# Causal-attention scores in row halves of the matmul array, with units taken in pairs over two PSUM banks

## The chip, the cores and the metric

The kernel runs on one core of a Trainium2 chip. The time is the device time of one execution in microseconds (us). Before the change three executions took 767.08, 772.93 and 774.23 us, median 772.93. Another execution was taken with the hardware profiler; it took 773.25 us, and the trace of it is what is read here.

## The reference

The input is `x`, 8 sequences of 512 tokens with 128 channels. Two layers follow each other, each of the form `x = x + s(xn) * silu(f(xn))` with `xn` the layernorm of `x`.

- First layer, `s`: causal attention with 16 heads of 8 channels. The latent forms of the weights fold, so that per head a score is `q . k / sqrt(8)` over 8 channels, a softmax over the keys up to the query follows, and the weighted sum of the values is the head's output. `f`: a mixture of 8 experts of 64 hidden channels (exact gelu), with the two best logits of each token as gates.
- Second layer, `s`: a recurrence over the tokens, `W = W - 0.01 (W k - v) k^T`, read with a query in each step, with its own layernorm, keys, values and queries. `f`: one matmul with the sign of the weight.

```python
attn = jnp.einsum('bhql,bkl->bhqk', q_lat, c_kv) / sqrt(hs)
attn = jnp.where(causal[None, None], attn, -jnp.inf)
attn = jax.nn.softmax(attn, axis=-1)
```

All is float32.

## The kernel before, in words

**Precision and the stacks.** The channels of q and k are split into three bf16 parts each. A score of a head is then one bf16 matmul whose contraction runs over 3 x 3 x 8 = 72 rows (each part of q against each part of k); these rows lie stacked in `qst` and `kst`, [128 rows, 16 heads, 512 tokens], two buffers each by the parity of the sequence. Rows 72 to 86 hold a coarse causal mask (of 32-token blocks) as products of two constant rows, and rows 96 to 98 hold ones in `kst` and, later, the negated row maximum in `qst`, again in three parts. The rows of a sequence get there over DRAM: q and k are written out from `parts` by SyncE (`write_parts`, pieces `q` and `k`), and read back by `load_stacks` in two halves of eight heads, 12 transfers each (issued at L445 for `qst` and L449 for `kst`). A half may be loaded once the exponential units that read the same buffer are far enough, and the wait for that stands on SyncE's queue.

**Two passes over the scores.** A pass computes the row maximum: `s_unit` (L804) takes rows 0 to 95 of the stacks, with 128 query tokens as weights and 128 or 256 keys as the moving side, and writes one 128x512 PSUM bank `ps_s`; `reduce` on VectorE (L1264) takes the maximum of it into `cand`. On the four units whose keys are the query block itself, four more matmuls (L808) add a triangular mask to the diagonal 32x32 blocks. `ps_s` has two banks, which units take by turns: the wait at the head of a unit is for the unit two before. When eight heads are through, `m_parts` and `m_rows` turn the maxima and bring them over DRAM into rows 96 to 98 of `qst`. The second pass, one sequence later, is `e_unit` (L786 writes the mask of the diagonal, L789 the score minus maximum over all 128 rows), transposed, so that keys lie on the partitions; ScalarE takes the exponential of a 128x512 bank of `ps_e` (L1069) into `prob`. `ps_e` also has two banks taken by turns.

**Values.** A group of four heads makes ten units of each pass, u = 0 to 9. Behind unit 3, 7 and 9 the values can be multiplied: `pv0`, `pv1` and `pv2` (L824) write 32 output rows for each of the four heads of `ps_v`, with a column of ones beside the values for the sum. Then `ps_v` is copied to `yT`, transposed back by `yt` (L831) into `ps_v`, and VectorE divides. There are four groups, called steps 0 to 3, so 40 units of each pass for a sequence.

**The order of the work.** Every engine runs its own instructions in the order that `run` and `iteration` (L336 to L361) give: for each step and each u, first `unit`, then the pieces that `PLAN` (L81) lists for it. In one iteration five sequences are in work: the projections and stack loads of the newest (`second`), the score pass and experts of the next (`nxt`), the exponentials, values and gating of the current (`cur`), and the second layer of the two before (`prev`, `older`). The last iteration has a plan of its own. The pieces of the second layer solve a triangular system by levels, `lev_a1`, `lev_d1` to `lev_d6` (L890 and L903; their results are copied by ScalarE at L1105, and multiplied by VectorE at L1319), go through the recurrence by blocks (`c_u`, `c_y`, `c_r`; L1338 is VectorE's step of `c_r`), and take their masks from GpSimd (L612, L614, L624; L1100 is the copy of the gram ahead of them). L1052 is the gelu of the experts. Between a piece on one engine and the piece on TensorE that waits for it lie whatever units the plan puts there. `prob` has ten buffers of 512 columns, one for each u.

```python
                for step in range(1 + max(at[0] for at in plan)):
                    for u in range(UNITS):
                        if step < GROUPS:
                            unit(cur, nxt, step, u)
                        for name in plan.get((step, u), []):
```

## Time and profile before

| | |
|---|---|
| median of three executions | 772.93 us |
| the profiled execution | 773.25 us, span 771.5 us |
| instructions | 14463 |
| TensorE, matmuls | 663.5 us busy, 86% |
| VectorE | 448.1 us, 58% |
| ScalarE | 369.3 us, 48% |
| GpSimd | 234.9 us, 30% |
| chain that ended last | TensorE 64%, VectorE 17%, DMA 6%, no wait that the profile shows 4%, ScalarE 4%, GpSimd 3% |
| read from and written to memory | 24.44 and 9.96 MB |

The profile is a page of totals over the whole span, and the trace behind it can be asked for windows, timelines and groups. Engines are called PE (TensorE matmul), PEld (its weight loads, which run beside it), DVE (VectorE), ACT (ScalarE), POOL (GpSimd) and SP (SyncE). A row of the costliest groups has the line of the program, the engine, the operation, out<-in, the number, then busy us, mean ns of one, and the idle time of the engine just before with what ended it. Matmuls are pipelined and their ends are modelled, so that what one holds the engine for is read from the start of the one behind it. The row of twelve or more instructions that a timeline gives as one spans from the start of the first to the end of the last.

### The profile page before, as it was taken

To read this page: it belongs to the slowest core of one execution; us is meant where nothing else is said; L and a number is where in the kernel's file an instruction comes from. 1 tells how busy PE (TensorE), PEld (TensorE's weight loads), DVE (VectorE), ACT (ScalarE), POOL (GpSimd) and SP (SyncE) were. 2 spreads that over 40 slices of the span, in tenths; PEclk is the share of its full clock that TensorE was granted. 3 is DMA by queue.
4 is the path that set the end of the run, shared out by engine and by line. 5 is a ranking of instruction groups with operands and counts; after the bars stand their busy time and mean duration, and the time that the engine had idled before them with its cause. 6 is when DMAs were issued, how large, how long until landed. Compare 5 with 4: busy or idle time off the path is not lost.

```text
span 771.5 us, 14463 instructions
## 1 busy us (share of the span) xinstructions
PE 663.5 (86%) x5682; PEld 458.5 (59%) x5734; DVE 448.1 (58%) x1044; ACT 369.3 (48%) x688; POOL 234.9 (30%) x356
## 2 busy tenths in 40 slices
PE   4177698979999899989998999899998998896875
PEld 2034365537666676657665876576666775555663
DVE  5466357555857576576758575758575654425331
ACT  3502346744556455644556455645564556571210
POOL 5703001222333153124404331423331502224431
PEclk9999889979999999999999999999999999999995
DMA  2732730450035102530044004400341000000000
GB/s 71 135 62 53 120 58 8 98 95 7 8 82 97 36 1 66 88 68 1 28 100 85 8 7 103 105 7 7 87 87 27 2 7 15 21 2 0 1 14 14
DMA packets 31283, 36.31 MB, mean 47 GB/s; under 512 B 4385, under 2 KB 26512, under 8 KB 31216
## 3 DMA queue, kind: packets, MB, share of 16 engines
q1 hardware_dynamic: 31216, 35.39, 22.1%
q8 instruction: 45, 0.74, 0.4%
q14 instruction: 22, 0.18, 0.1%
HBM read 24.44 MB, written 9.96 MB: 45 GB/s over the span
## 4 chain that ended last, share of the span: by engine, by line
PE 64%; DVE 17%; DMA 6%; issue 4%; ACT 4%; POOL 3%; SPq 2%; another core or an unknown queue 0%; POOLq 0%; DVEq 0%; ACTq 0%
PE ps_s L804 8%; PE ps_v L824 8%; PE ps_e L789 5%; DVE cand L1264 5%; DMA kst<-split_scratch 4%; PE ps_a L749 4%; PE ps_e L786 4%; PE ps_c L890 3%; PE ps_c L903 3%; PE ps_a L738 3%; PE ps_a L713 3%; PE ps_s L808 2%; DVE stats L1195 2%; PE ps_c L907 2%; DVE second L1209 2%
## 5 line engine op out<-in xcount | busy, mean ns | idle before, releaser
L1264 DVE TENSOR_REDUCE cand<-ps_s 128x4 f32<-128x512 f32 (+1 forms) x320 | 212.9, 683 | 94.0 <-PE ps_s L808 73.8
L1069 ACT ACTIVATE prob<-ps_e 128x512 f32<-128x512 f32 x320 | 188.2, 597 | 136.8 <-PE ps_e L789 97.2
L804 PE MATMUL ps_s<-kst,qst 96*128 96x128 bf16 (+1 forms) x1024 | 134.2, 249 | 41.8 <-DMA kst<-split_scratch 23.6
L804 PEld LDWEIGHTS ps_s<-kst,qst 96*128 96x128 bf16 x1024 | 81.0, 105 | 100.7 <-issue 52.4
L789 PE MATMUL ps_e<-qst,kst 128*128 128x128 bf16 (+3 forms) x460 | 104.5, 296 | 0.0
L824 PE MATMUL ps_v<-prob,vaug 128*32 128x512 f32 (+3 forms) x1024 | 89.0, 443 | 0.3
L786 PE MATMUL ps_e<-identb,negmask 128*128 128x256 bf16 (+1 forms) x320 | 83.3, 260 | 6.0 <-ACT prob L1069 5.8
L624 POOL TENSOR_TENSOR second<-second,upmask 128x512 f32<-128x512 f32 x42 | 53.1, 1274 | 34.6 <-PE ps_c L890 34.6
L789 PEld LDWEIGHTS ps_e<-qst,kst 128*128 128x128 bf16 x512 | 50.6, 99 | 5.6 <-issue 0.3
L587 POOL CAST mparts<-nm 128x32 bf16<-128x32 f32 x16 | 3.4, 212 | 157.9 <-DVE nm L1271 157.9
L890 PE MATMUL ps_c<-second 128*128 128x128 f32 x336 | 46.0, 280 | 1.0 <-DVE second L1319 1.0
L786 PEld LDWEIGHTS ps_e<-identb,negmask 128*128 128x128 bf16 x320 | 31.2, 97 | 23.0 <-ACT prob L1069 11.9
L890 PEld LDWEIGHTS ps_c<-second 128*128 128x128 f32 x336 | 41.7, 191 | 4.4 <-DVE second L1319 1.8
L824 PEld LDWEIGHTS ps_v<-prob,vaug 128*32 128x32 f32 x1024 | 23.5, 108 | 31.1 <-issue 23.5
L903 PE MATMUL ps_c<-second 128*128 128x128 f32 x280 | 38.5, 281 | 2.9 <-ACT second L1105 2.2
L903 PEld LDWEIGHTS ps_c<-second 128*128 128x128 f32 x280 | 34.8, 191 | 9.1 <-issue 6.3
L612 POOL TENSOR_TENSOR second<-second,lowmask 128x512 f32<-128x512 f32 x7 | 8.9, 1273 | 101.0 <-ACT second L1100 101.0
L738 PE MATMUL ps_a<-xnT,w1s 128*128 128x512 f32 x64 | 36.9, 659 | 0.7 <-DVE krest L1215 0.3
L749 PE MATMUL ps_a<-w2s,hid 128*128 128x128 f32 x256 | 35.3, 281 | 1.0 <-ACT mrow L1061 1.0
L1048 ACT ACTIVATE hid<-ps_a,vecT 128x512 f32<-128x512 f32 x32 | 22.0, 688 | 24.0 <-PE ps_a L738 24.0
L749 PEld LDWEIGHTS ps_a<-w2s,hid 128*128 128x128 f32 x256 | 31.4, 191 | 1.7 <-ACT mrow L1061 1.7
L808 PE MATMUL ps_s<-negmask,identb 32*32 32x128 bf16 x512 | 31.4, 236 | 0.0
(301 smaller groups left out, 1076.6 us busy)
## 6 DMA issues: line engine op xcount, KB each, us to landing
qst<-split_scratch SPq DMA_DIRECT2D x48, 192.0 KB
kst<-split_scratch SPq DMA_DIRECT2D x144, 64.0 KB
split_scratch<-qparts SPq DMA_DIRECT2D x8, 384.0 KB, 2.5
split_scratch<-kparts SPq DMA_DIRECT2D x8, 384.0 KB, 2.5
xn<-in_L_attn_x_dram SPq DMA_DIRECT2D x8, 256.0 KB, 3.1
x_res<-in_L_attn_x_dram SPq DMA_DIRECT2D x8, 256.0 KB, 6.8
out_dram<-second SPq DMA_DIRECT2D x7, 256.0 KB, 2.4
max_scratch<-mrow SPq DMA_DIRECT2D x16, 96.0 KB, 1.7
```

The lines of the kernel that those rows point to most:

```text
L624: g.tensor_tensor(r.pair_up[lv % 2][:, :, :], r.gram[:, :, :], bcast(upmask[:, lv, :], 1, NT), ALU.mult)\
L738: mm(ps_a[:, :], w1s[:, 2 * c:2 * c + 2, :].rearrange("p e f -> p (e f)"), xnT[b.parity][:, :], start=True, stop=True)\
L749: mm(ps_a[:, tok(i)], hid[:, c, tok(i)], w2s[:, c, :], start=(i == 0 and c == 0), stop=False, skip_group_check=True)
L786: mm(diag, negmask[:, :], bcast(identb[:, :], 1, len(todo)), start=True, stop=False, skip_group_check=True)
L789: last = mm(ps_e[:, bank, at:at + TOK - P * j], k[:, hd, tok(j)], q[:, hd, P * j:TOK], start=False, stop=True, skip_group_check=True)
L804: last = mm(ps_s[:, bank, w * n:w * (n + 1)], q[0:MAXROW, hd, tok(i)], k[0:MAXROW, hd, keys[0]:keys[1]], start=(n == 0), stop=True, skip_g ...
L808: last = mm(ps_s[lo:lo + FINE, bank, :].rearrange("p (a c) -> p a c", a=GH)[:, :, lo:lo + FINE], identb[0:FINE, 0:FINE], bcast(negmask[0:F ...
L824: last = mm(ps_v[32 * hh:32 * hh + 32, P * j:TOK], vaug[:, j, GH * grp + hh, :], prob[:, u, o:o + TOK - P * j], start=(j == 0), stop=(j == ...
L890: last = mm(r.ps_c0[:, tok(i)], r.pair_up[lv % 2][:, i, :], r.inv[:, i, :], start=True, stop=True)
L903: last = mm(r.ps_c0[:, tok(i)], r.invT[:, i, :], r.ablk[:, i, :], start=True, stop=True)
L1069: af(prob[:, u, :], ps_e[:, u % 2, :], ACT.Exp).then_inc(S["e_emptied"], 1)
L1264: vec.tensor_reduce(cand[:, i, h0:h0 + len(hds), S_SLOT[u]], ps_s[:, u % 2, :].rearrange("p (a c) -> p a c", a=len(hds)), AX_X, ALU.max)\
```

## The change

Scores of the row-maximum pass no longer take the coarse mask rows, so 72 rows of contraction remain; 64 of them are given to one half of the array's rows and the other 8 dropped from the pass (they stay in the stacks for the second pass). The 16 heads are split into two sides. A head of side 0 has its rows from row 0 up, a head of side 1 from row 64 up and around (`(64 + 8 * pair) % 128`), and the matmul of the pass contracts rows 0 to 63 for side 0 and 64 to 127 for side 1. A pair of units, one for four heads of side 0 and one for four heads of side 1, fills the two banks of `ps_s` with matmuls that alternate between the sides, and one reduction reads both banks. The pass has 20 pairs for a sequence instead of 40 units. The diagonal mask is added as two matmuls of 64 rows for each side and bank (`half_of`), over 64 or 128 columns of four heads, with constants that are also stored with their halves swapped (`ident_swap`, `neg_swap`, four transfers at the start).

The second pass goes in pairs too: `e_pair` fills both banks of `ps_e`, over all 128 rows, and one exponential reads both. For both passes the wait at the head of a pair is for the pair before. A fill of `ps_v` holds eight heads: each group of 32 output rows takes a head of side 0 and then one of side 1 of the same rows, whose weights have their values in other columns (0 to 8 and 16 to 24 of the 32). So there are two fills, six pieces and two `yt` for a sequence. Pairs run at even u only, and the plan puts the pieces anew. `load_stacks` has 25 transfers for a half instead of 12, of half the bytes or less; the loads of the row maxima are two for a half instead of one. The value copy on ScalarE is two copies, and `prob` has 6 buffers of 1024 columns.

In the diff the lines that are taken out of `load_stacks`, `e_unit`, `s_unit`, `pv` and `yt` are left out, since the kernel before is printed above.

```diff
-PAIRS = PARTS * PARTS * HD
-FINE = 32
 MAXROW = 96
+HALF = P // 2
 HALF_HEADS = 8
-GROUPS, GH = 4, 4
-UNITS = 10
+FILLS, SIDES, GH = 2, 2, 4
+FH, FW = 8, 16
+STEPS, UNITS = 4, 10
+UNIT_PAIRS = FILLS * UNITS
+PROB_RING = 6
+ONES_AT = (96, 32)
 ONES = 1 + 0x3F80 / 2 ** 23
...
 PLAN = {
     (0, 0): ["c_y2"], (0, 1): ["c_r3", "gb0"], (0, 2): ["ln2_stats", "c_u3"], (0, 3): ["c_y3"], (0, 4): ["gb1", "ln2_norm"],
-    (0, 6): ["pv0", "c_xn2t", "ln3_stats", "c_out", "gb2"], (0, 7): ["ln3_norm"], (0, 8): ["gb3"], (0, 9): ["pv1", "c_ht"],
-    (1, 0): ["load_x", "c_kt", "c_qt", "m_rows1"], (1, 1): ["c_vk", "out"], (1, 2): ["c_gram", "pv2"], (1, 3): ["logits"],
-    (1, 4): ["yt", "c_ffn", "gates"], (1, 5): ["lev_a1"], (1, 6): ["pv0"], (1, 7): ["lev_d1"], (1, 8): ["gt"],
-    (1, 9): ["pv1", "lev_a2"], (2, 0): ["ln1_stats", "lev_d2", "m_parts0"], (2, 2): ["ln1_norm", "lev_a3", "pv2"], (2, 3): ["lev_d3"],
-    (2, 4): ["yt", "m_rows0", "zero"], (2, 5): ["lev_a4", "xnt"], (2, 6): ["pv0", "q", "lev_d4"], (2, 8): ["lev_a5", "k"],
-    (2, 9): ["pv1", "lev_d5"], (3, 0): ["stacks0", "h0"], (3, 1): ["lev_a6"], (3, 2): ["h1", "lev_d6", "pv2"], (3, 3): ["c_u0"],
-    (3, 4): ["h2", "yt", "c_y0"], (3, 5): ["c_r1"], (3, 6): ["pv0", "c_u1"], (3, 7): ["c_y1", "h3"], (3, 8): ["c_r2"],
-    (3, 9): ["pv1", "c_u2"], (4, 0): ["m_parts1", "gelu", "stacks1"], (4, 1): ["pv2"], (4, 2): ["v"], (4, 3): ["yt", "x1"],
+    (0, 6): ["c_xn2t", "ln3_stats", "c_out", "gb2"], (0, 7): ["ln3_norm"], (0, 8): ["pv0", "gb3"], (0, 9): ["c_ht"],
+    (1, 0): ["load_x", "c_kt", "c_qt", "m_rows1"], (1, 1): ["c_vk", "out"], (1, 2): ["c_gram"], (1, 3): ["logits"],
+    (1, 4): ["c_ffn", "gates"], (1, 5): ["lev_a1"], (1, 6): ["pv1"], (1, 7): ["lev_d1"], (1, 8): ["gt"],
+    (1, 9): ["lev_a2"], (2, 0): ["pv2", "ln1_stats", "lev_d2", "m_parts0"], (2, 2): ["yt", "ln1_norm", "lev_a3"], (2, 3): ["lev_d3"],
+    (2, 4): ["m_rows0", "zero"], (2, 5): ["lev_a4", "xnt"], (2, 6): ["q", "lev_d4"], (2, 8): ["pv0", "lev_a5", "k"],
+    (2, 9): ["lev_d5"], (3, 0): ["stacks0", "h0"], (3, 1): ["lev_a6"], (3, 2): ["h1", "lev_d6"], (3, 3): ["c_u0"],
+    (3, 4): ["h2", "c_y0"], (3, 5): ["c_r1"], (3, 6): ["pv1", "c_u1"], (3, 7): ["c_y1", "h3"], (3, 8): ["c_r2"],
+    (3, 9): ["c_u2"], (4, 0): ["pv2", "m_parts1", "gelu", "stacks1"], (4, 2): ["v"], (4, 3): ["yt", "x1"],
 }
 LAST_PLAN = {
     (0, 0): ["last:zero_state", "c_y2"], (0, 1): ["c_r3"], (0, 2): ["gb0", "ln2_stats", "c_u3"], (0, 3): ["c_y3"], (0, 4): ["gb1"],
...
+def head_of(fill, side, hh):
+    return FH * fill + SIDES * hh + side
+def slot_of(fill, side, hh):
+    return HALF_HEADS * side + GH * fill + hh
+def low_rows(side):
+    return slice(HALF * side, HALF * side + HALF)
...
             def iteration(second, nxt, cur, prev, older, plan=PLAN):
                 for step in range(1 + max(at[0] for at in plan)):
                     for u in range(UNITS):
-                        if step < GROUPS:
-                            unit(cur, nxt, step, u)
+                        if step < STEPS and u % 2 == 0:
+                            unit(cur, nxt, step // 2, UNITS // 2 * (step % 2) + u // 2)
...
                                 if name in ("pv0", "pv1"):
-                                    pieces[name](of, step)
+                                    pieces[name](of, step // 2)
                                 elif name in ("pv2", "yt"):
-                                    pieces[name](of, step - 1)
+                                    pieces[name](of, (step - 1) // 2)
...
+            for dst, src in ((ident_swap, identb), (neg_swap, negmask)):
+                for side in range(SIDES):
+                    sp.dma_start(dst[low_rows(side), :], src[low_rows(1 - side), :]).then_inc(S["swap_loaded"], 16)
...
             def load_stacks(b, half):
...
                 loaded = S[f"stack_loaded{half}"]
...
+                sp.wait_ge(S[f"stack_zeroed{b.parity}"], 6)
+                after(sp, S["e_filled"], b.count(UNIT_PAIRS, UNIT_PAIRS * (half - 3) // 2))
                 sp.wait_ge(S["scratch_written"], b.count(32, 32))
...
+                q_rows = scratch[0].rearrange("r (d h) q -> (r d) (h q)", d=HD)
+                k_rows = scratch[1].rearrange("r (d h) q -> (r d) (h q)", d=HD)
                 n3 = PARTS * HD
...
+                for side in range(SIDES):
+                    s0 = slot_of(half, side, 0)
+                    heads, span = slice(s0, s0 + GH), slice(TOK * s0, TOK * (s0 + GH))
+                    for lo, n, first in STACK_ROWS[side]:
+                        sp.dma_start(qst[b.parity][lo:lo + n, heads, :].rearrange("p h q -> p (h q)"), q_rows[first:first + n, span],
                                      max_dma_last_dim=4096).then_inc(loaded, 16)
+                    for pair in range(PARTS * PARTS):
+                        lo, s = (HALF * side + HD * pair) % P, pair // PARTS
+                        sp.dma_start(kst[b.parity][lo:lo + HD, heads, :].rearrange("p h q -> p (h q)"), k_rows[HD * s:HD * s + HD, span],
+                                     max_dma_last_dim=4096).then_inc(loaded, 16)
...
+            def unit(cur, nxt, fill, u):
                 if nxt is not None:
...
+                    s_pair(nxt, fill, u)
                 if cur is not None:
...
+                    e_pair(cur, fill, u)
+            def half_of(plain, swapped, a, side):
+                return (plain if a == side else swapped)[low_rows(side), :]
+            def e_pair(b, fill, u):
                 q, k = qst[b.parity], kst[b.parity]
...
+                after(pe, S["e_emptied"], b.count(UNIT_PAIRS, UNITS * fill + u))
+                if u == 0:
+                    pe.wait_ge(S["mrow_loaded"], b.count(64, 32 * fill + 32))
                 todo = [(u, 0, 0)] if u < 4 else [(u - 4, 1, 0), (u - 4, 3, 384)] if u < 8 else \
                     [(2 * (u - 8), 2, 0), (2 * (u - 8) + 1, 2, 256)]
...
+                apart = 3 if u < 8 else 2
+                for side in range(SIDES):
+                    diag = ps_e[:, side, :].rearrange("p (n c) -> p n c", c=P)[:, 0:apart * (len(todo) - 1) + 1:apart, :]
+                    mm(diag, negmask[:, :], bcast(identb[:, :], 1, len(todo)), start=True, stop=False, skip_group_check=True)
+                    for hh, j, at in todo:
+                        slot = slot_of(fill, side, hh)
+                        last = mm(ps_e[:, side, at:at + TOK - P * j], k[:, slot, tok(j)], q[:, slot, P * j:TOK],
+                                  start=False, stop=True, skip_group_check=True)
                 last.then_inc(S["e_filled"], 1)
...
+            def s_pair(b, fill, u):
                 q, k = qst[b.parity], kst[b.parity]
...
+                after(pe, S["s_emptied"], b.count(UNIT_PAIRS, UNITS * fill + u))
+                if u == 0:
+                    pe.wait_ge(S[f"stack_loaded{fill}"], b.count(STACK_LOADED, STACK_LOADED))
                 i, keys, hds = S_UNIT[u]
+                w = keys[1] - keys[0]
                 for n, hh in enumerate(hds):
...
+                    for side in range(SIDES):
+                        rows, slot = low_rows(side), slot_of(fill, side, hh)
+                        last = mm(ps_s[:, side, w * n:w * (n + 1)], q[rows, slot, tok(i)], k[rows, slot, keys[0]:keys[1]],
+                                  start=(n == 0), stop=True, skip_group_check=True)
                 if u < NT:
...
+                    for a in range(2):
+                        for side in range(SIDES):
+                            last = mm(ps_s[:, side, :].rearrange("p (n c) -> p n c", n=GH)[:, :, HALF * a:P],
+                                      half_of(identb, ident_swap, a, side),
+                                      bcast(half_of(negmask, neg_swap, a, side)[:, HALF * a:P], 1, GH), start=False, stop=True,
+                                      skip_group_check=True)
                 last.then_inc(S["s_filled"], 1)
...
+            def pv(b, fill, piece):
                 if piece == 0:
...
+                    after(pe, S["v_emptied"], b.count(2 * FILLS, 2 * fill))
+                    if fill == 0:
+                        pe.wait_ge(S["v_ready"], b.count(1, 1))
                         pe.wait_ge(S["a_emptied"], b.count(A_FILLS, a_number(b, A_V) + 1))
...
+                pe.wait_ge(S["e_emptied"], b.count(UNIT_PAIRS, UNITS * fill + (4, 8, 10)[piece]))
                 for j, u0, at in (((0, 0, 0),), ((1, 4, 0), (3, 4, 384)), ((2, 8, 0),))[piece]:
...
+                    for side in range(SIDES):
+                        for hh in range(GH):
+                            u, o = (u0 + hh, at) if j != 2 else (u0 + hh // 2, 256 * (hh % 2))
+                            last = mm(ps_v[32 * hh:32 * hh + 32, P * j:TOK], vaug[:, j, head_of(fill, side, hh), :],
+                                      prob[:, u % PROB_RING, side, o:o + TOK - P * j], start=(j == 0 and side == 0),
+                                      stop=(j == 2 and side == SIDES - 1), skip_group_check=True)
                 last.then_inc(S["pv_used"], 1)
...
+            def yt(b, fill):
+                pe.wait_ge(S["v_emptied"], b.count(2 * FILLS, 2 * fill + 1))
                 for i in range(NT):
                     last = tr(ps_v[:, tok(i)], yT[:, tok(i)], ident[:, :])
...
             def v(b):
                 a_full(b, A_V)
-                after(act, S["pv_used"], b.count(3 * GROUPS, 0))
-                copy(vaug[:, :, :, 0:HD], ps_a[:, :].rearrange("p (i h d) -> p i h d", i=NT, h=HEADS))\
-                    .then_inc(S["a_emptied"], 1)
+                after(act, S["pv_used"], b.count(3 * FILLS, 0))
+                by_turn = ps_a[:, :].rearrange("p (i h t d) -> p i h t d", i=NT, t=FILLS, d=HD)
+                copy(vaug[:, :, 0:HEADS:FILLS, 0:HD], by_turn[:, :, :, 0, :]).then_inc(S["v_ready"], 1)
+                copy(vaug[:, :, 1:HEADS:FILLS, FW:FW + HD], by_turn[:, :, :, 1, :]).then_inc(S["a_emptied"], 1)
...
+            def unit(cur, nxt, fill, u):
                 if cur is None:
                     return
-                act.wait_ge(S["e_filled"], cur.count(GROUPS * UNITS, UNITS * grp + u + 1))
-                if u in (0, 4, 8):
-                    after(act, S["pv_used"], cur.count(3 * GROUPS, 3 * (grp - 1) + u // 4 + 1))
-                af(prob[:, u, :], ps_e[:, u % 2, :], ACT.Exp).then_inc(S["e_emptied"], 1)
-            def pv(b, grp):
-                if grp == GROUPS - 1:
+                act.wait_ge(S["e_filled"], cur.count(UNIT_PAIRS, UNITS * fill + u + 1))
+                if u in PROB_FREED:
...
-            def unit(cur, nxt, mgrp, u):
+            def unit(cur, nxt, fill, u):
                 if nxt is None:
                     return
                 i, keys, hds = S_UNIT[u]
-                if mgrp == 0 and u == 0:
+                if fill == 0 and u == 0:
                     after(dve, S["nm_ready"], nxt.count(2, 0))
-                dve.wait_ge(S["s_filled"], nxt.count(GROUPS * UNITS, UNITS * mgrp + u + 1))
-                h0 = GH * mgrp + hds[0]
-                vec.tensor_reduce(cand[:, i, h0:h0 + len(hds), S_SLOT[u]],
-                                  ps_s[:, u % 2, :].rearrange("p (a c) -> p a c", a=len(hds)), AX_X, ALU.max)\
+                dve.wait_ge(S["s_filled"], nxt.count(UNIT_PAIRS, UNITS * fill + u + 1))
+                of_sides = cand[:, i, FH * fill:FH * fill + FH, S_SLOT[u]].rearrange("p (t h) -> p t h", t=SIDES)
+                vec.tensor_reduce(of_sides[:, :, hds[0]:hds[0] + len(hds)],
+                                  ps_s[:, :, :].rearrange("p t (a c) -> p t a c", a=len(hds)), AX_X, ALU.max)\
                     .then_inc(S["s_emptied"], 1)
             def m_parts(b, half):
...
+PROB_FREED = {0: -1, 2: 0, 6: 1}
+STACK_ROWS = (
+    ((0, 24, 0), (24, 24, 0), (48, 24, 0)),
+    ((64, 24, 0), (88, 24, 0), (112, 16, 0), (0, 8, 16)))
+STACK_LOADED = 16 * (len(STACK_ROWS[0]) + len(STACK_ROWS[1]) + SIDES * PARTS * PARTS)
```

## Rows read from the trace of the kernel before

**Rows 1.** The page: span, and busy time of TensorE and VectorE (share, instructions).
```profile
span 771.5 us, 14463 instructions
...
PE 663.5 (86%) x5682; PEld 458.5 (59%) x5734; DVE 448.1 (58%) x1044; ACT 369.3 (48%) x688; POOL 234.9 (30%) x356
```

**Rows 2.** Windows: us, busy us of each engine (instructions), granted clock, DMA share, GB/s.
```profile
41.20:77.70 36.50, 29.48 (x179) 15.44 (x180) 25.59 (x58) 4.32 (x14) 7.91 (x16) 1.00 0.29 54
...
95.40:160.40 65.00, 56.06 (x527) 34.02 (x532) 37.13 (x82) 37.40 (x67) 11.34 (x22) 0.95 0.31 60
...
323.50:340.60 17.10, 13.65 (x134) 8.62 (x135) 15.84 (x44) 10.84 (x17) 8.07 (x9) 1.00 0.48 94
340.60:385.30 44.70, 43.11 (x403) 33.33 (x407) 27.86 (x66) 21.99 (x47) 17.86 (x24) 1.00 0.05 16
385.30:405.50 20.20, 20.09 (x175) 13.27 (x176) 10.10 (x20) 11.87 (x21) 0.92 (x4) 1.00 0.43 99
...
669.00:695.90 26.90, 25.71 (x219) 14.06 (x220) 6.47 (x16) 20.38 (x37) 5.02 (x4) 1.00 0.01 2
```

**Rows 3.** Timeline of TensorE: an unmasked unit and a pv piece.
```profile
361.89 0.40 PE L804 MATMUL ps_s<-kst,qst 96*128 96x128 bf16 x4
362.12 0.28 PE L786 MATMUL ps_e<-identb,negmask 128*128 128x256 bf16 x1
...
362.55 1.07 PE L824 MATMUL ps_v<-prob,vaug 128*32 128x384 f32 x16
363.55 0.38 PE L890 MATMUL ps_c<-second 128*128 128x128 f32 x1
```

**Rows 4.** Timeline of TensorE, a masked unit.
```profile
366.23 0.39 PE L804 MATMUL ps_s<-kst,qst 96*128 96x128 bf16 x4
366.54 0.23 PE L808 MATMUL ps_s<-negmask,identb 32*32 32x128 bf16 x4
366.71 0.23 PE L786 MATMUL ps_e<-identb,negmask 128*128 128x128 bf16 x1
...
366.99 0.39 PE L804 MATMUL ps_s<-kst,qst 96*128 96x128 bf16 x4
```

**Rows 5.** The page: reduction and exponential of one unit (busy, mean ns, idle before).
```profile
L1264 DVE TENSOR_REDUCE cand<-ps_s 128x4 f32<-128x512 f32 (+1 forms) x320 | 212.9, 683 | 94.0 <-PE ps_s L808 73.8
L1069 ACT ACTIVATE prob<-ps_e 128x512 f32<-128x512 f32 x320 | 188.2, 597 | 136.8 <-PE ps_e L789 97.2
```

**Rows 6.** Groups by form, 300 to 400 us: other sizes on both engines.
```profile
L1052 ACT ACTIVATE hid<-hid 128x2048 f32<-128x2048 f32 x1 | 1.9, 1910 | 0.0
...
L1319 DVE TENSOR_TENSOR second<-second,ps_c 128x256 f32<-128x256 f32 x6 | 2.5, 410 | 1.6 <-PE ps_c L903 1.5
```

**Rows 7.** Timeline: a level matmul group and the ACT copy behind it; a VectorE step.
```profile
387.71 1.05 PE L890 MATMUL ps_c<-second 128*128 128x128 f32 x8
...
388.80 0.37 ACT L1105 COPY second<-ps_c 128x256 f32<-128x256 f32 x1 [0.29 <-PE ps_c L890]
...
401.68 0.28 DVE L1338 SCALAR_TENSOR_TENSOR rhs<-ps_c,vk 128x128 f32<-128x128 f32 x1
```

**Rows 8.** Timeline: the ACT copy of the gram and its GpSimd masks.
```profile
350.97 0.59 ACT L1100 COPY second<-ps_c 128x512 f32<-128x512 f32 x1 [0.29 <-PE ps_c L875]
...
354.21 2.51 POOL L624 TENSOR_TENSOR second<-second,upmask 128x512 f32<-128x512 f32 x2
```

**Rows 9.** Timeline of TensorE in the first score stage, without exponential units.
```profile
42.93 0.61 PE L804 MATMUL ps_s<-kst,qst 96*128 96x128 bf16 x4
...
44.57 0.61 PE L804 MATMUL ps_s<-kst,qst 96*128 96x128 bf16 x4
...
46.72 1.24 PE L804 MATMUL ps_s<-kst,qst 96*128 96x256 bf16 x4 [0.15 <-DVE cand L1264]
...
48.12 1.24 PE L804 MATMUL ps_s<-kst,qst 96*128 96x128 bf16 x8 [0.15 <-DVE cand L1264]
```

**Rows 10.** Timeline of the SP queue: issue of three stack loads.
```profile
388.24 0.97 SPq L449 DMA_DIRECT2D kst<-split_scratch  x3
```

160 lines of the change are left out of this document (53 added, 107 removed), and 9 rows, old and new, of the table LAST_PLAN.

## The prediction

> **What bounds the kernel now.** I read the page first, then the busy time by windows, then the timelines of single stages. The page gives TensorE 86% of the span and no other engine above 59% [rows 1]. The windows say where that holds. From 160 to 651 us the kernel repeats one stretch six times; the one shown, 323.5 to 405.5, is 82.0 us long. Its first 17.1 us (step 0 of the plan) are not TensorE's: VectorE is busy 15.8 of them. The next 44.7 us and the last 20.2 us are TensorE's, busy 43.1 and 20.1 [rows 2]. Outside the six, the stage of 41.2 to 77.7 us has score units of the first sequence and no exponential units, and it ends in a chain to the stack loads of the second sequence. The stage of 669 to 695.9 us has exponential units and no score units; ScalarE is busy 20.4 of 26.9 us and TensorE 25.7 [rows 2]. Behind it lies a tail of the second layer that the change does not touch.
>
> **TensorE's work in a level stretch (82 us).** All per sequence, 40 units before, 20 pairs after.
> - Score stream. Four matmuls of 128 columns with their own weights take 0.23 us until the next instruction, 0.055 us each [rows 3]: 40 x 0.22 = 8.8 us. No row shows two 64-row halves at once. Bounds: in turn, 8.8 again; together, 4.4. Nearest are the diagonal masks, four 32-column strips of 128 columns each, which with the switch behind them take 0.17 us instead of 4 x 0.055 plus a switch [rows 4]: they run together. I take together, 4.4, and keep the other end as a rival.
> - Masks. A masked unit goes from score to exponential in 0.48 us [rows 4], an unmasked one in 0.23 [rows 3]: 0.25 x 16 = 4.0 us, nearly all of it two switches of the array's split (four matmuls take 0.31 us before the masks instead of 0.22, so about 0.095 a switch). After: 512 + 256 columns for each half, 6 x 0.055 = 0.33 us for 8 pairs, 2.6 us together, 5.2 in turn.
> - Switches. Every pair now enters and leaves the halved form: 20 x 2 x 0.095 = 3.8 us. Bounds 0 and 4; the row is of another split, and I take it.
> - pv pieces: the same streams, 6 pieces instead of 12, each with two switches (one piece holds the engine 1.00 us [rows 3]): -1.1 us. Transposes of yT: 8 matmul records fewer at 0.11 (eight of that size take 0.89 us [rows 7]): -0.9 us. The exponential units' matmuls stay.
> Sum: -8.8 - 4.0 - 1.1 - 0.9 + 4.4 + 2.6 + 3.8 = -4.0 us.
>
> The Trainium skill, "TensorE: Matmul & The Clock Gate", LDWEIGHTS section, has a load of P columns take P/1.2 ns, 107 ns for 128; if the loads of the two halves did not overlap, a pair's eight loads would take 0.85 us instead of 0.22, and the stretch would be 12.6 us longer, not 4.0 shorter. The trace has four loads and matmuls in 0.23 us [rows 3], so I don't use it.
>
> **What replaces it.** A reduction of one unit takes 683 ns, an exponential 597 [rows 5]. The slopes are (683 - 410) / 256 = 1.07 ns a column on VectorE and (1910 - 597) / 1536 = 0.855 on ScalarE [rows 5, 6], so a pair takes 1.23 and 1.04 us: 0.14 and 0.16 us less than two units, 3 us per sequence on each. But before, two banks let TensorE fill one while the other was read; now it fills both and waits for both. A bare masked pair turns round in 0.74 (stream, masks, switches) + 0.2 + 1.23 + 0.05 = 2.2 us, an unmasked one in 1.9, on the exponential side 0.65 + 0.2 + 1.04 + 0.06 = 1.95. In a level stretch there are 4.1 us of TensorE for each pair, so this seldom shows there. What does show is the plan: pieces of odd u now follow those of even u with no unit between. By hand, slot by slot with these durations:
> - Step 0: TensorE starts at 0; reductions, c_y2, c_r3, gb0, ln2, c_y3, gb1, the norm of 2.3 us, ln3, gb2, ln3's norm run on VectorE in that order; c_kt comes at 18.7 us instead of 17.1, with 12 units done instead of 11 (worth 0.5). Net +1.1.
> - c_kt to the end of lev_d5: 42.5 us against 44.7 [rows 2]. 39.3 are work. Waits are 3.2: lev_a1 1.3, since the copy of the gram and three GpSimd masks of 1.27 us (L612, L614 and the first of L624's two) must end first, at 355.5 (354.21 and half of 2.51), 4.5 us after that copy began [rows 8], and a pv piece, a transpose and a unit no longer stand between; lev_a3 to lev_d3 0.6 (drain 0.2, copy 0.37 [rows 7], handovers); the rest xnt and the reduction after ln1's norm.
> - Step 3 and the end: work 17.7; lev_d6 to c_u0 0.75, c_y0 to c_r1 0.45, c_u1 to c_y1 0.5, c_r2 to c_u2 0.85 (a VectorE step of 0.28 [rows 7] behind a pair's reduction). 20.2 us, as now.
> 81.4 us against 82.0: -0.6, six times, -3.6 us. So 3.4 of the 4.0 us of work come back as TensorE waiting: 5.2 us are idle now (82.0 less 13.65, 43.11 and 20.09 [rows 2]; switches and handovers hide in the rest, and by the starts of its instructions I count some 7), and 10 to 11 then.
>
> **The other stages.**
> - First score stage: TensorE is on the lower of its two levels in these records (masked units start 1.64 us per two, unmasked 1.40 [rows 9]; the windows' granted clock of 1.00 does not show it). A masked pair there: 0.43 + 0.64 + 0.2 + 1.23 = 2.5 us, an unmasked 1.95. Step 0: +4; step 1, with logits and gates: +1; step 2 up to k's write: +1. Sum +6, all on the path, since the stack loads wait for k.
> - Second stage (95.4 to 160.4): the out group and pieces hide most; +0.5.
> - Exponentials without scores (669 to 695.9): five to eight pairs stand bare at 1.95 us instead of 1.2. Slot by slot it is 33.5 us instead of 26.9, and lev_a1 now also waits for pv2: +6.5.
> - Stack loads: 25 issues for a half instead of 12, at 0.34 us each [rows 10], 8.5 us instead of 4.1. Bytes are the same. The first of them are issued at 388.2 [rows 10], and the first score unit that needs them starts the next stretch at 405.5, 17 us later; of these the slower issue takes 4.4, so I take 0 and keep the rest as a rival. SP's later loads wait 4 us more, and are needed far later. The coarse loads and their GpSimd and VectorE work before 41 us vanish, the zeroing in halves and the four swap loads come: 0, between -1 and +1. v's copy in two on ScalarE, 0.1 us, lies beside TensorE.
> Sum: -3.6 + 6 + 0.5 + 6.5 = +9.4. The profiled execution took 773.25 us (span 771.5), 0.3 above the median of 772.93. 773.25 + 9.4 = 782.
>
> The Trainium skill, "TensorEngine Tiling (Array Packing)", PSUM Bottleneck, warns that tiling speeds up TensorE and not the reading of PSUM, which may then become the bound. By that rule step 0 and the first score stage gain nothing from the halves, which is what the hand schedule has; VectorE's 15.8 of 17.1 us [rows 2] agree.
>
> **Rivals.**
> - A, the forecast: halves run together, single filling and missing cover give it back. 773 to 791. Chance 0.52.
> - B, faster: the waits between pieces hide each other, because VectorE and ScalarE queues are shorter (3 us each). Against: the round trips are latency, not load. It decides if TensorE's waits stay near today's 7 us per stretch (5.2 of them plain idle): 3 us more gained, six times, 782 - 19 = 763. Chance 0.22.
> - C, slower by much: the halves run in turn. 4.4 + 2.6 = 7.0 us more per stretch, of which 2.4 fall in step 0 behind VectorE: 4.6 x 6 = 28, and 5 in the first stage: 815. For it: no row shows row halves; against: the strips in rows 4. Chance 0.12.
> - D: the slower issue makes the stacks land late, so that each stretch starts 2 us late: 794. Against: the 17 us of slack, and a stretch that already hides these loads whole. Chance 0.06.
> Something else, 0.08, on both sides.
>
> **Numbers.** About 1% (765.2 to 780.7) is what a measurement of this kernel can tell from no change. Faster: 0.17 of B and 0.04 of the rest, 0.21. Same: 0.24 of A, 0.05 of B, 0.04, 0.33. Slower: 0.28 of A, C and D, 0.46. The range takes in A, the near side of B and D, and part of the way to C: 764 to 804.
>
> **What would show it.** Right: score matmuls of the two halves start a few ns apart and a pair's eight take near 0.25 us; reductions of 1.2 and exponentials of 1.04 us; a stretch of 81 to 82 us with TensorE waiting 10 to 12 of it, at lev_a1, lev_d3, c_u0 and c_u2; k's first write near 84 us instead of 77.7; the last exponential stage near 33 us. Wrong: a stretch under 79 or over 84 us, eight score matmuls in 0.45 us or more, or score units that wait for a DMA in the level stretches.

## The result, and the profile after

The changed kernel takes 783.31 us (781.57 to 784.35, four executions) where the kernel before takes 770.22: ratio 1.0158, 95% interval 1.0123 to 1.0193. It is slower, by about 1.6%. The forecast was 782, range 764 to 804, with slower as the likeliest side (0.46). The total was hit, but by terms that were wrong in both directions, so its closeness is luck; this is the part to learn from. A few executions are clearly slower than the others of the same kernel, and they are left out of all medians and ratios below.

The page of the changed kernel: its span, busy times and the costliest exponential and reduction, which answer to [rows 1, 5].

```profile
span 782.6 us, 13636 instructions
...
PE 634.1 (81%) x5383; PEld 408.4 (52%) x5414; DVE 432.5 (55%) x856; ACT 335.7 (43%) x522; POOL 231.9 (30%) x353
...
L1086 ACT ACTIVATE prob<-ps_e 128x1024 f32<-128x1024 f32 x160 | 163.7, 1023 | 189.7 <-PE ps_e L797 189.4
L1285 DVE TENSOR_REDUCE cand<-ps_s 128x8 f32<-128x1024 f32 (+1 forms) x160 | 194.5, 1216 | 68.9 <-PE ps_s L812 35.9
```

Every engine does less than before: TensorE 29 us, VectorE 16, ScalarE 34. The span is 11.1 us longer. So it went into waits, and the page can't say where.

The windows of the changed kernel, cut at the same events as [rows 2]: the first score stage to the write of k; the three parts of one level stretch; and the last exponential stage with its granted clock (third column from the end; before 80.4 us the trace holds no record of the clock, so the 1.00 of the first row says nothing).

```profile
37.40:78.70 41.30, 23.95 (x158) 10.37 (x154) 24.64 (x43) 4.32 (x14) 8.36 (x18) 1.00 0.13 39
...
319.52:337.85 18.33, 13.77 (x129) 7.13 (x131) 16.13 (x39) 9.52 (x12) 8.56 (x12) 1.00 0.30 84
337.85:381.54 43.69, 41.37 (x386) 30.36 (x387) 27.21 (x54) 19.75 (x36) 16.35 (x23) 1.00 0.05 16
381.54:402.62 21.08, 19.15 (x161) 11.84 (x160) 8.91 (x13) 10.85 (x15) 1.86 (x4) 1.00 0.34 97
...
651.20:669.00 17.80, 13.85 (x60) 6.27 (x60) 8.28 (x27) 7.60 (x9) 5.77 (x7) 0.62 0.10 29
669.00:707.30 38.30, 28.31 (x258) 18.80 (x260) 4.89 (x11) 19.47 (x23) 6.74 (x7) 1.00 0.01 4
```

A level stretch is 83.1 us instead of 82.0. Taken by the starts of reductions and exponentials (first reduction of sequence 0 at 42.2 before and 38.1 after, and so on), the 11.1 us of span come from these stages:

| stage | before | after | difference | forecast |
|---|---|---|---|---|
| start to the first reduction | 42.2 | 38.1 | -4.1 | 0 |
| first reduction of sequence 0 to that of 1 | 54.2 | 56.9 | +2.7 | +6 |
| sequence 1 to sequence 2 | 65.0 | 62.3 | -2.7 | +0.5 |
| from there to the first exponential of the last sequence | 489.9 | 495.1 | +5.2 | -3.6 |
| that to the end of the last exponential | 44.3 | 54.9 | +10.6 | +6.5 |
| tail | 75.9 | 75.3 | -0.6 | 0 |
| sum | 771.5 | 782.6 | +11.1 | +9.4 |

The halves do what they promise. TensorE's timeline of a masked pair in the changed kernel, to set beside [rows 3, 4]:

```profile
367.88 0.40 PE L812 MATMUL ps_s<-kst,qst 64*128 64x128 bf16 x8
368.12 0.38 PE L817 MATMUL ps_s<-negmask,identb 64*128 64x512 bf16 x1
368.12 0.48 PE L817 MATMUL ps_s<-neg_swap,ident_swap 64*128 64x512 bf16 x2
368.33 0.27 PE L817 MATMUL ps_s<-negmask,identb 64*128 64x256 bf16 x1
368.54 0.50 PE L794 MATMUL ps_e<-identb,negmask 128*128 128x128 bf16 x2
```

Eight score matmuls hold the engine for 0.24 us (367.88 to 368.12), where four took 0.23, and the masks of both halves start together at 368.12. The Trainium skill, "TensorEngine Tiling (Array Packing)", Key Properties, says that different tiles work in parallel and that a change of mode drains TensorE. The trace agrees on the first, with the 0.24 us. On the second it shows a price: behind the last masks, of 256 columns, the first matmul of the full array starts after 0.21 us (368.33 to 368.54), and behind a 256-column matmul without a change the next one starts after 0.12 (362.12 to 362.24 in the kernel before), so about 0.09 us is the change.

What TensorE waits for in that stretch, changed kernel first, then the kernel before (us in total, times, longest):

```profile
PE ps_c L952 <- ACT u_sb L1133: 1.4, 2, 1.0
PE ps_c L853 <- DVE second L1230: 1.3, 1, 1.3
PE ps_s L812 <- DVE cand L1285: 1.3, 4, 0.5
PE ps_c L903 <- issue: 0.9, 1, 0.9
PE ps_c L942 <- DVE second L1346: 0.7, 1, 0.7
...
```

```profile
PE ps_s L804 <- DVE cand L1264: 1.6, 3, 1.1
PE ps_c L840 <- DVE second L1209: 1.2, 1, 1.2
PE ps_a L743 <- DVE hid L1248: 0.9, 1, 0.9
PE ps_e L786 <- ACT prob L1069: 0.6, 1, 0.6
PE ps_c L855 <- ACT second_flat L1085: 0.4, 1, 0.4
```

The second list is whole, 4.7 us; the first goes on with six of 0.4 to 0.6 to 8.5. Its L853 and L812 are the L840 and L804 of the kernel before, with waits of about the same size. The new ones are dependent steps of the second layer, L903 (lev_a1), L942 and L952 (c_u, c_y), that ran behind a unit before.

### The profile page after: what moved, and what is told of

Same layout as the page of the kernel before. It is cut to its first block, busy times and chain, and to the rows that moved or that the text cites. A ratio compares the mean times of both kernels' runs of the same rounds, so it can differ in the third digit from the quotient of the medians.

```text
span 782.6 us, 13636 instructions
## 1 busy us (share of the span) xinstructions
PE 634.1 (81%) x5383; PEld 408.4 (52%) x5414; DVE 432.5 (55%) x856; ACT 335.7 (43%) x522; POOL 231.9 (30%) x353
## 3 DMA queue, kind: packets, MB, share of 16 engines
q1 hardware_dynamic: 32484, 34.48, 15.4%
## 4 chain that ended last, share of the span: by engine, by line
PE 60%; DVE 16%; ACT 7%; issue 7%; POOL 4%; SPq 3%; DMA 2%; POOLq 0%; DVEq 0%
PE ps_v L836 7%; DVE cand L1285 6%; PE ps_e L797 6%; PE ps_s L812 5%; PE ps_e L794 4%; PE ps_c L903 4%; PE ps_a L757 4%; PE ps_c L916 4%; PE ps_a L746 3%; PE ps_a L721 2%; ACT prob L1086 2%; SPq L463 2%; DVE second L1230 2%; PE ps_c L920 2%; POOL rstd L564 2%
## 5 line engine op out<-in xcount | busy, mean ns | idle before, releaser
L1086 ACT ACTIVATE prob<-ps_e 128x1024 f32<-128x1024 f32 x160 | 163.7, 1023 | 189.7 <-PE ps_e L797 189.4
L1285 DVE TENSOR_REDUCE cand<-ps_s 128x8 f32<-128x1024 f32 (+1 forms) x160 | 194.5, 1216 | 68.9 <-PE ps_s L812 35.9
L797 PE MATMUL ps_e<-qst,kst 128*128 128x384 bf16 (+3 forms) x481 | 104.5, 301 | 0.0
L812 PE MATMUL ps_s<-kst,qst 64*128 64x128 bf16 (+1 forms) x1024 | 67.7, 245 | 42.2 <-DVE cand L1285 26.8
L794 PE MATMUL ps_e<-identb,negmask 128*128 128x256 bf16 (+1 forms) x320 | 83.2, 260 | 13.2 <-ACT prob L1086 10.9
L836 PE MATMUL ps_v<-prob,vaug 128*32 128x256 f32 (+3 forms) x1024 | 81.1, 446 | 2.2 <-ACT prob L1086 2.2
L812 PEld LDWEIGHTS ps_s<-kst,qst 64*128 64x128 bf16 x1024 | 30.8, 98 | 89.4 <-DVE cand L1285 55.9
L633 POOL TENSOR_TENSOR second<-second,upmask 128x512 f32<-128x512 f32 x42 | 52.9, 1268 | 33.6 <-PE ps_c L903 33.6
L903 PE MATMUL ps_c<-second 128*128 128x128 f32 x336 | 47.0, 283 | 9.4 <-issue 5.5
L903 PEld LDWEIGHTS ps_c<-second 128*128 128x128 f32 x336 | 41.2, 191 | 20.7 <-issue 14.8
L836 PEld LDWEIGHTS ps_v<-prob,vaug 128*32 128x32 f32 x1024 | 27.9, 110 | 38.8 <-issue 32.5
L817 PE MATMUL ps_s<-negmask,identb 64*128 64x512 bf16 (+1 forms) x128 | 34.9, 354 | 0.0
L817 PE MATMUL ps_s<-neg_swap,ident_swap 64*128 64x512 bf16 (+1 forms) x128 | 34.3, 354 | 0.0
```

Source lines behind the costliest of these rows:

```text
L633: g.tensor_tensor(r.pair_up[lv % 2][:, :, :], r.gram[:, :, :], bcast(upmask[:, lv, :], 1, NT), ALU.mult)\
L794: mm(diag, negmask[:, :], bcast(identb[:, :], 1, len(todo)), start=True, stop=False, skip_group_check=True)
L797: last = mm(ps_e[:, side, at:at + TOK - P * j], k[:, slot, tok(j)], q[:, slot, P * j:TOK], start=False, stop=True, skip_group_check=True)
L812: last = mm(ps_s[:, side, w * n:w * (n + 1)], q[rows, slot, tok(i)], k[rows, slot, keys[0]:keys[1]], start=(n == 0), stop=True, skip_group ...
L817: last = mm(ps_s[:, side, :].rearrange("p (n c) -> p n c", n=GH)[:, :, HALF * a:P], half_of(identb, ident_swap, a, side), bcast(half_of(ne ...
L836: last = mm(ps_v[32 * hh:32 * hh + 32, P * j:TOK], vaug[:, j, head_of(fill, side, hh), :], prob[:, u % PROB_RING, side, o:o + TOK - P * j] ...
```

## The experiments

All ratios are against the kernel before, run on the same chip. The length of a level stretch is the distance between the first exponentials of two successive sequences.

### Order of issue inside a pair

```diff
-                for n, hh in enumerate(hds):
-                    for side in range(SIDES):
+                for side in range(SIDES):
+                    for n, hh in enumerate(hds):
```

> The changed kernel, but the four score matmuls of side 0 are issued before the four of side 1, so that only two at the border can run side by side; the masks stay as they are. Theory 1 (the two row halves really run at once, and TensorE's own time still counts in the level stretches): a pair's score stream goes from about 0.23 to about 0.42 us, 0.19 x 20 = 3.8 us a sequence, of which the step behind VectorE hides a quarter: +2.8 us in each of six stretches and 3 in the first score stage, about 803 us. Theory 2 (TensorE waits for reductions and pieces anyway, its own time is free): under +5 us, 783 to 788.

783.84 us, ratio 1.0147 (1.0110 to 1.0184): the same as the changed kernel. It says nothing on either theory, for the edit did not take the concurrency away. The eight matmuls of TensorE's timeline still last 0.24 us:

```profile
367.16 0.41 PE L812 MATMUL ps_s<-kst,qst 64*128 64x128 bf16 x8
367.40 0.38 PE L817 MATMUL ps_s<-negmask,identb 64*128 64x512 bf16 x1
```

Their starts come in twos 14 ns apart (3 ns in the changed kernel), and each of the two series goes on at about 55 ns, which is the distance of matmuls on the same rows [rows 3]. The trace does not name the half that a matmul used. Read as the two halves, the first matmul of side 1 starts 14 ns after the first of side 0, although three more of side 0 stand ahead of it in the program.

### Concurrency taken away

```diff
-                for n, hh in enumerate(hds):
-                    for side in range(SIDES):
-                        rows, slot = low_rows(side), slot_of(fill, side, hh)
+                for side in range(SIDES):
+                    for n, hh in enumerate(hds):
+                        rows, slot = (slice(0, MAXROW), low_rows(1))[side], slot_of(fill, side, hh)
```

> The changed kernel with the concurrency of the halves taken away: the four score matmuls of side 0 use rows 0 to 95, which is the full array, then the four of side 1 use rows 64 to 127; masks and the number of switches stay. (In the run with the sides issued in turn the trace still had matmuls of both halves starting 14 ns apart, so that one took nothing away.) A pair's eight go from about 0.23 to about 0.44 us, 4.2 us of TensorE a sequence. Theory 1 (TensorE's own time counts outside the step that VectorE bounds): a level stretch of 83.1 grows to 85.5 or more, 800 us. Theory 2 (TensorE waits for other engines between pieces, and they take its own time in): a level stretch stays under 84, 783 to 789 us.

813.40 us, ratio 1.0531 (1.0484 to 1.0577). Theory 1 holds and by more than it said. The timeline has five score matmuls from 382.69 and three more from 383.08, and between them the first mask:

```profile
382.69 0.55 PE L812 MATMUL ps_s<-kst,qst 96*128 96x128 bf16 x5
383.02 0.39 PE L817 MATMUL ps_s<-negmask,identb 64*128 64x512 bf16 x1
383.08 0.33 PE L812 MATMUL ps_s<-kst,qst 64*128 64x128 bf16 x3
```

The program has the mask (L817) behind all eight score matmuls (L812), and it starts ahead of three of them: it works on the rows of side 0, they on those of side 1. So a little concurrency is left in this run too. The level stretch is 86.4 us. Running the score matmuls at once is worth 3.3 us a stretch, and 30 us in all. TensorE's own time does count; it was not being absorbed.

### Exponential side bank by bank

```diff
-                after(pe, S["e_emptied"], b.count(UNIT_PAIRS, UNITS * fill + u))
+                after(pe, S["e_emptied"], b.count(2 * UNIT_PAIRS, 2 * (UNITS * fill + u) + side - 1))
...
-                af(prob[:, u % PROB_RING, :, :], ps_e[:, :, :], ACT.Exp).then_inc(S["e_emptied"], 1)
+                for side in range(SIDES):
+                    act.wait_ge(S["e_filled"], cur.count(2 * UNIT_PAIRS, 2 * (UNITS * fill + u) + side + 1))
...
+                    af(prob[:, u % PROB_RING, side, :], ps_e[:, side, :], ACT.Exp).then_inc(S["e_emptied"], 1)
```

> The changed kernel, but the exponential side goes bank by bank again: the matmuls of side 1 follow those of side 0, each bank has its own exponential (about 0.6 us instead of one of 1.02) and is refilled when that bank alone is free. Places in the order and the score pairs stay. Theory 1 (filling both banks and waiting for both is what costs): the stretch without score units, 55 us in the changed kernel from the first exponential of the last sequence to its last, comes down to about 46, and a level stretch of 83.1 to about 82: 768 us. Theory 2 (it is the order, pieces of odd u without a unit ahead of them): a level stretch stays within 0.3 us of 83.1, and only the last stage gains, 3 to 5 us: 779 us.

772.35 us, ratio 1.0000 (0.9977 to 1.0023). The last stage falls from 54.9 to 45.1 us, nearly the 44.3 of the kernel before. The level stretch stays at 82.9 to 83.3. So each theory is right in its own place: filling both exponential banks costs about 10 us where no score units stand between (2.4 of them by way of the clock, see the run with fillers below), and nothing that shows where they do. The bare pairs of the changed kernel show why. Its timeline:

```profile
698.94 0.28 PE L794 MATMUL ps_e<-identb,negmask 128*128 128x256 bf16 x1 [1.12 <-ACT prob L1086]
...
699.81 1.02 ACT L1086 ACTIVATE prob<-ps_e 128x1024 f32<-128x1024 f32 x1 [0.92 <-PE ps_e L797]
...
700.88 0.28 PE L794 MATMUL ps_e<-identb,negmask 128*128 128x256 bf16 x1 [1.12 <-ACT prob L1086]
```

A pair comes round every 1.94 us; TensorE and ScalarE take turns at idling.

### The same, with a unit ahead of every piece

```diff
-                        if step < STEPS and u % 2 == 0:
-                            unit(cur, nxt, step // 2, UNITS // 2 * (step % 2) + u // 2)
+                        if step < STEPS:
+                            unit(cur, nxt, step // 2, UNITS // 2 * (step % 2) + u // 2, u % 2)
...
+                if nxt is not None and side == 0:
+                    s_pair(nxt, fill, u)
+                if cur is not None:
+                    e_unit(cur, fill, u, side)
```

> As before this one, bank by bank on the exponential side, and now the unit of side 0 stands at even u and that of side 1 at odd u, so that each piece has exponential units ahead of it on TensorE; the score pairs stay at even u. Theory 1: little more than the bank-by-bank kernel gives, within 3 us of it. Theory 2 (the order): a level stretch falls to 81 or less, since the waits at lev_a1, c_u0, c_y1 and c_u2 of 0.7 to 1.5 us are covered by 0.33 us of matmuls each: 6 x 2 = 12 us less than the bank-by-bank kernel, about 760 us with it.

765.19 us, ratio 0.9907 (0.9880 to 0.9934). Faster than both kernels. The level stretch is 82.0 in three of four (83.3 in the other), 1 us less than bank by bank at even u; the forecast of 81 or less was too hopeful. So the order costs. The stretches of 82.0 us have 3.4 us of step 0 at 1.2 GHz and the one of 83.3 has 6.8; in the changed kernel only the first of the four has any (3.4 us, in a stretch of 83.2 where the others take 83.1). So some of the gain may go to the clock, which no run shows by itself.

### The order alone, in the kernel before

```diff
-                        if step < GROUPS:
+                        if step < GROUPS and u % 2 == 0:
                             unit(cur, nxt, step, u)
+                            unit(cur, nxt, step, u + 1)
```

> The kernel before, with its own units, banks by turns and pieces, but units u and u + 1 stand together at even u, as the pairs of the changed kernel do. Theory 2 (the order costs): a level stretch goes from 82.0 to 83.5, 779 us. Theory 1 (only the filling of both banks costs): 770 us, level stretch 82.0 to 82.4.

783.67 us, ratio 1.0160 (1.0131 to 1.0188): theory 2, with 83.9 us a stretch. Nothing but the places of the units changed, no instruction more or less, and the waits of the changed kernel appear, the second and third of these:

```profile
PE ps_c L841 <- DVE second L1210: 1.1, 1, 1.1
PE ps_c L940 <- ACT u_sb L1117: 1.0, 2, 0.6
PE ps_c L891 <- DVE second L1320: 1.0, 1, 1.0
```

L940 is c_y and L891 lev_a1 in that kernel; L841 is the L840 of the kernel before, where it waits 1.2 us.

### Both score banks filled at once, in the kernel before

```diff
                 if nxt is not None:
                     s_unit(nxt, grp, u)
+                    s_unit(nxt, grp, u + 1)
...
-                after(pe, S["s_emptied"], b.count(GROUPS * UNITS, UNITS * grp + u - 1))
+                if u % 2 == 0:
+                    after(pe, S["s_emptied"], b.count(GROUPS * UNITS, UNITS * grp + u))
```

(VectorE reduces units u and u + 1 one after the other, once both are filled.)

> The kernel before with units u and u + 1 together at even u, as in the run of that kind (783.7 us, level stretch 83.9), and now the score side also fills both banks before either is reduced and waits for both reductions; the exponential side keeps its banks by turns, and there are no halves. Theory 1 (filling both score banks at once costs beyond the order): the level stretch grows from 83.9 to 85.5 or more, 793 us or more, which is the rest of what the changed kernel pays. Theory 2 (the order alone is the cost): 83.9 to 84.3, 784 to 786 us.

807.78 us, ratio 1.0462 (1.0415 to 1.0509): theory 1, level stretch 85.6. Of the 28.8 us between the spans of the two profiled executions 10.7 are the level stretches and 15.4 the first two stages (62.4 and 71.3 us against 52.9 and 65.4), where score units have few others beside them. The whole stretch of each kernel in the windows view, in this order: before, order alone, both banks, concurrency taken away, changed.

```profile
408.90:490.80 81.90, 76.76 (x711) 55.23 (x714) 53.73 (x130) 44.61 (x83) 26.78 (x38) 1.00 0.24 52
```

```profile
412.20:496.10 83.90, 77.58 (x710) 55.64 (x714) 53.70 (x129) 44.48 (x84) 26.86 (x38) 1.00 0.23 51
```

```profile
435.30:520.90 85.60, 78.07 (x710) 55.52 (x714) 53.77 (x129) 43.03 (x84) 26.81 (x38) 1.00 0.22 50
```

```profile
419.00:505.40 86.40, 79.38 (x679) 53.12 (x675) 52.27 (x105) 40.04 (x63) 26.77 (x37) 1.00 0.17 50
```

```profile
405.50:488.60 83.10, 74.27 (x672) 49.32 (x674) 52.27 (x105) 40.10 (x63) 26.76 (x38) 1.00 0.17 51
```

It reads as a ladder: +1.9 for the order, +1.7 for filling both score banks (the two score units also stand side by side in that run, ahead of both exponential units, and what that costs by itself was not tried), +0.8 for all else in the pairs, -3.3 for the halves at once, +1.1 together (82.0 to 83.1). Each step is one kernel against the next, so their sum is fixed; that each keeps its size in other company was not tried.

### Matmuls that keep TensorE busy in the last stage

```diff
                 if cur is not None:
+                    if nxt is None and fill == 0 and 1 <= u <= 4:
+                        pe.wait_ge(S["s_emptied"], SEQS * UNIT_PAIRS)
+                        for _ in range(3):
+                            mm(ps_s[:, 0, :], identb[:, :], kst[cur.parity][:, 0, :], start=True, stop=True, skip_group_check=True)
                     e_pair(cur, fill, u)
```

> The changed kernel with three matmuls of 512 columns ahead of each of four exponential pairs in the first step of the last iteration, into a free bank that nobody reads; they fall where TensorE stands idle between 652 and 668 us. Theory 1 (the granted clock of 0.5 from 654 to 667 us, after that idling, costs about 3 us of the last stage): the clock stays at 1.0, the last stage goes from 55 to about 52 us, 780 us. Theory 2 (the last stage waits for ScalarE and VectorE whatever the clock): 783 us or up to 2 more.

778.81 us, ratio 1.0092 (1.0063 to 1.0121). Twelve matmuls more, and the last stage is shorter, 52.5 us instead of 54.9. The windows view of it:

```profile
648.20:665.00 16.80, 13.05 (x93) 7.53 (x94) 8.49 (x26) 8.34 (x10) 7.27 (x10) 1.00 0.14 37
665.00:701.70 36.70, 27.85 (x242) 16.96 (x240) 4.90 (x11) 18.48 (x21) 5.00 (x4) 0.95 0.01 2
```

The granted clock is 1.00 where the changed kernel had 0.62 in the same part (651.2 to 669.0, shown above). Cut finer, the changed kernel shows what went ahead of that, idling, and a stay at the lower level, 1.2 GHz, behind it:

```profile
652.00:654.00 2.00, 0.47 (x4) 0.34 (x5) 0.14 (x1) 1.46 (x2) 1.28 (x2) 0.97 0.00 0
654.00:656.00 2.00, 1.58 (x6) 0.95 (x4) 1.08 (x4) 1.18 (x2) 0.00 (x0) 0.50 0.45 131
656.00:666.00 10.00, 8.62 (x36) 2.98 (x36) 5.00 (x14) 3.07 (x3) 3.77 (x4) 0.50 0.09 26
```

The lower level was worth 2.4 us, as far as this run separates it. The trace has it for 13.7 us in the changed kernel (653.9 to 667.5). In the kernel before, TensorE is as idle (busy 0.07 us between 650 and 652), then busy for 2.00 of the next 2 us and again of the 2 after them, and there the lower level lasts 3.4 us. Of the 5.4 us between the two spans 3.2 lie ahead of sequence 2, which starts at 154.1 instead of 157.3; up to there the two programs are the same, so this much a start differs by without a cause in the program.

### Finer stack loads, in the kernel before

```diff
-                heads = slice(HALF_HEADS * half, HALF_HEADS * (half + 1))
...
+                for part in range(2):
+                    h0 = HALF_HEADS * half + GH * part
+                    heads, span = slice(h0, h0 + GH), slice(TOK * h0, TOK * (h0 + GH))
```

(and within a part the three loads of `qst` now stand ahead of the nine of `kst`, where before each of `qst` was followed by three of `kst`)

> The kernel before with its stack loads alone cut finer: a half of the stacks is 24 transfers of four heads instead of 12 of eight, same bytes. Theory 1 (the finer transfers are why the stacks of sequences 1 and 2 land 2.4 and 4.7 us sooner after the write of k in the changed kernel): those two waits shrink by as much, 765 us. Theory 2 (the slower issue counts, or the sooner landing comes of the other things that changed): 770 to 774 us.

758.69 us, ratio 0.9828 (0.9799 to 0.9857). The largest gain of any single edit here, and beyond theory 1. The first reductions of sequences 0, 1 and 2 are at 37.9, 87.3 and 147.7 instead of 42.2, 96.4 and 161.4: 4.3, 4.8 and 4.6 us, each at a wait for these loads. The rest is unchanged (level stretch 82.0). From the write of k to the next sequence, kernel before and then this one:

```profile
77.70:96.40 18.70, 11.23 (x64) 5.97 (x64) 7.32 (x13) 7.70 (x8) 0.91 (x4) 0.89 0.74 123
141.70:161.40 19.70, 14.36 (x134) 8.33 (x133) 7.94 (x16) 13.27 (x18) 3.44 (x6) 0.98 0.65 115
```

```profile
73.30:87.30 14.00, 10.34 (x65) 5.80 (x64) 7.29 (x12) 7.62 (x8) 0.91 (x4) 0.94 0.42 135
133.80:147.70 13.90, 13.90 (x135) 8.20 (x133) 7.78 (x15) 11.12 (x16) 0.91 (x4) 1.00 0.45 137
```

The two columns at the end are the share of the DMA engines and GB/s. From the first issue to the last landing, a first half of the stacks, the same bytes, takes 14.5, 15.0 and 16.0 us in the kernel before and 10.3, 10.1 and 10.4 here. The packets are of 4096 bytes in both; one takes 0.40 us on average in the second of these loads before and 0.20 here, in keeping with engines that are busy 0.42 of the time instead of 0.74. Two things can be told apart in the traces. The rate is higher, 121 to 130 GB/s of such packets against 99 to 106. And while the first half is on its way 1.3 MB of them move instead of 1.5, since the second half, whose first issue follows that of the first half after 8.5 us instead of 4.4, gets less in its way. By these numbers the first is worth 2 to 3 us and the second about 2 of the 4 to 6 us saved, an estimate that no run separates. So the slower issue, counted as a cost in the prediction, seems to help here. Why the rate is higher is open, and the size and the order of the transfers were not tried apart. The Trainium skill, "DMA: Bandwidth & Descriptors", Measured, has the rule to batch, and calls transfers under 64 KB dominated by their descriptors; it measured transfers over 128 partitions issued from GpSimd. Here, over 8 partitions and issued from SyncE, 32 KB transfers of `kst` beat those of 64 KB, and the measurement decides.

### No coarse mask, in the kernel before

```diff
-                    for lo in range(0, P, FINE):
-                        last = mm(ps_s[lo:lo + FINE, bank, :].rearrange("p (a c) -> p a c", a=GH)[:, :, lo:lo + FINE],
-                                  identb[0:FINE, 0:FINE], bcast(negmask[0:FINE, 0:FINE], 1, GH), start=False, stop=True,
-                                  skip_group_check=True)
+                    last = mm(ps_s[:, bank, :].rearrange("p (a c) -> p a c", a=GH), identb[:, :], bcast(negmask[:, :], 1, GH),
+                              start=False, stop=True, skip_group_check=True)
```

(and the coarse rows, their loads and the waits for them are gone)

> The kernel before without the coarse mask rows and their loads; the diagonal mask is one matmul of 128 rows over 512 columns (0.21 us, no switch of the array's split) in place of four 32-row strips with two switches. Theory 1 (the coarse loads hold up the start, which is the 4.1 us that the changed kernel starts its first score unit sooner): the first reduction at about 38 instead of 42 us, level stretches within 0.3 us of 82.0, 766 us. Theory 2 (the start hangs on the weight preparation): the first reduction stays at 42 us, 770 us.

766.70 us, ratio 0.9929 (0.9907 to 0.9952). The time is as theory 1 had it, the place is not: the first reduction is at 41.1, 1.1 us sooner and not 4. Level stretches are 81.6, 0.4 less each, and 3.3 us lie between the first reductions of sequences 0 and 2, which is about what a start differed by between two kernels with the same first stages (3.2, above).

### Both together

> The kernel before with both of the single changes that helped it: the finer stack loads (758.7 us) and the diagonal mask as one full matmul without the coarse rows (766.7 us). Theory 1 (they save in different places, the prologue's two waits and 0.4 us of switches in each level stretch): 754 us. Theory 2 (the gain of the full mask was the prologue's too, and is already had): 758 us.

754.98 us, ratio 0.9767 (0.9740 to 0.9794). Theory 1. It is the fastest kernel of the study, with the units and the order of the kernel before: full array, banks by turns.

### Work moved into or out of step 0

Both start from the kernel with a unit at every u (765.19 us). In the first, two of the five score pairs of step 0 go to step 1; in the second, four exponential units come into step 0 as well.

```diff
+S_AT = {at: divmod(n, UNITS) for n, at in enumerate([(0, 0), (0, 2), (0, 6)] + [(1, u) for u in (0, 2, 3, 4, 6, 7, 8)] + [(s, u) for s in (2, 3) for u in range(0, UNITS, 2)])}
```

> The changed kernel with exponential units bank by bank at every u (765.2 us, level stretch 82.0), and two of the five score pairs of step 0 moved to step 1. Theory 1 (step 0 is VectorE's, 16.0 of 18.2 us busy, and its length is the sum of its queue): 2.4 us of reductions leave it, step 0 falls by 2 us and the rest of the stretch grows by the pairs' 1.5 us or less: 81 us, 759 us. Theory 2 (the chain of layernorms sets step 0, reductions run in its gaps): nothing gained in step 0, 767 us or more.

> As the one before, and four exponential units of the 40 move from steps 2 and 3 into step 0, where TensorE and ScalarE stand idle. Theory 1: 4 x 0.33 us less in the part that TensorE bounds, a level stretch about 1.3 us shorter than with the score pairs moved alone, 751 us. Theory 2 (in steps 2 and 3 TensorE waits between dependent pieces, so units that leave uncover waits there): under 0.5 us a stretch, 757 us or more.

776.45 us, ratio 1.0049 (1.0030 to 1.0067), and 763.25 us, ratio 0.9901 (0.9872 to 0.9931). Theory 1 on step 0 falls: with 2.4 us of reductions out of it, the step shrinks by 0.35 (first score matmul at 401.84 to the first key projection at 419.85, 18.0 us, against 395.50 to 413.86, 18.4), and the rest of the stretch grows by 0.9 (64.6 against 63.6), so that a level stretch is 82.6 to 84.0 us. That is what theory 2 says of step 0. Sequence 1 to 2 takes 63.5 us instead of 59.3; that the doubled score pairs of step 1 stand bare there is argued, not shown. In the second half of step 0 TensorE is partly at the lower level in the kernel that they start from and in the first of the two. Windows view, in that order:

```profile
404.00:413.90 9.90, 7.75 (x55) 3.00 (x52) 8.62 (x21) 3.74 (x7) 3.32 (x5) 0.83 0.22 59
```

```profile
411.00:421.00 10.00, 8.15 (x52) 3.69 (x53) 7.46 (x19) 3.65 (x7) 2.71 (x4) 0.83 0.19 54
```

The changed kernel has 1.00 in its step 0. How long the lower level lasts goes with the length of a stretch. In the first of the two, stretches with 3.4 us of it take 82.6 and 82.9 us and one with 6.8 takes 84.0; in the second, a stretch without it takes 80.8 and those with 3.4 take 81.8 to 82.2. In the bank-by-bank kernel and the changed one it shows less: 83.0 and 83.3 with 3.4 us of it against 82.9 without, and 83.2 against 83.1. The exponential units in step 0 give 13 us back, but against the start of the two, 765.19, that is 2 us, with ratios whose intervals overlap. Stretch for stretch it is 0.7 to 2.2 us shorter than with the score pairs moved alone, which is theory 1 of that run (1.3); its 751 us do not come, since they built on a time for the first of the two that it missed.

## Why the prediction was right, and where it was not

- **The halves run at once, streams of 0.055 us.** Right: eight in 0.24 us. The concurrency is worth 3.3 us a level stretch for the score matmuls alone, and the kernel without it takes 813.4 us, where rival C had priced 815 (it counted the masks in turn too, which this kernel does not do). The pair's reduction of 1216 ns and exponential of 1023 are as forecast (1.23 and 1.04 us).
- **A level stretch, -0.6 us.** This is a step that failed: it is +1.1. By [rows 2] and the windows above TensorE is busy 76.85 before and 74.29 after, -2.6 where -4.0 was forecast. The ends of matmuls are modelled, so the split between work and wait is soft, the net of +1.1 is not. Counted from each start to the next, the matmuls that the change touches (into `ps_s`, `ps_e` and `ps_v`) hold TensorE 6.1 us less, more than the 4.0, and all the others 3.6 us more. Idle time behind one of those others stands at 14 places instead of 2. So one reading is that the work went down by more than forecast and that a wait at a dependent step costs more than its idle time shows; it was not tested.
- **Added waits, 3.4 us a stretch.** Right, and they stand where they were placed: idle time goes from 5.2 to 8.8, with lev_a1 at 0.9 (forecast 1.3), lev_d3 0.55 (0.6), c_u0 0.7 (0.75), c_r1 0.4 (0.45), c_y1 0.4 (0.5) and c_u2 0.5 (0.85). Step 0 took 18.3 us. The forecast nets it to 18.2 in its text and puts it at 18.7 in its sum: with 18.2 the parts would give 80.9, not 81.4. The middle was forecast at 42.5 and took 43.7, the end at 20.2 and took 21.1; these two are where the stretch misses, though none of the idle times just listed is above its forecast. What was set too low there is the 39.3 and 17.7 us of work (busy 41.4 and 19.2). From sequence 2 to the last sequence the sum is -3.6 forecast, +5.2 measured. Of the signs named in advance, the stretch of 81 to 82 us and the 10 to 12 us of waiting did not come.
- **Rival B**, that the waits hide each other, is refuted by the idle time and by the run that moved the units alone: 1.9 us more a stretch with the same instructions.
- **The last stage, +6.5.** Right for the stretch that I worked out, 669 to the end, and the few us ahead of it: the steps behind L853 (L840 before) took 40.5 us (666.9 to 707.4) against 33.9 before. Wrong in leaving out what lies ahead of it, 651 to 669, where TensorE stands idle for a wide exponential (busy 0.47 of 2 us) and is then at the lower level for 13.7 us. The kernel before has 0.90 there, the changed one 0.62, and the run with fillers prices it at 2.4 us.
- **Stack loads, 0 with a rival that they cost.** This is the other step that failed, and by its sign. I counted the slower issue (25 at 0.34 us) and looked at the level stretches, where they are hidden and were hidden still. I did not ask what finer transfers do where the loads are on the path, in the first two stages, which [rows 2] show with the DMA engines busy 0.29 and 0.31 over a stage that ends in a wait for them. In the kernel before, the finer loads alone save 13.8 us. That the changed kernel's loads do the same is read from the same starts (38.1 and 37.9) and landings (11.0 to 12.2 us from first issue to last landing of a first half, against 14.5 to 16.0) and not from a run of its own, since its layout has no coarser form.
- **The first stage, +6.** Measured from the first reduction to the write of k: 35.5 before, 40.6 after, +5.1. Right, and for the reason given: masked pairs come 2.57 us apart there (forecast 2.5), and the eight score matmuls take 0.40 us instead of 0.24, the lower level that the forecast had read from [rows 9]. But k is written at 78.7 us and not near 84, since the stacks of the first sequence landed sooner.

The errors sum up as follows, by the table: the three stages up to sequence 2 came out 10.6 us below their forecast, mostly by the loads as it seems, the level stretches 8.8 above and the last stage 4.1 above. That +9.4 met +11.1 is luck. The pairs themselves cost about 25 us against a kernel before with equally fine loads (783.31 to 758.69), and the loads that came with them paid half of it back.

## What to carry to other kernels

Before an edit that joins two fills into one, list for every piece what stood between it and the piece that it waits for: here an order with the same instructions cost 1.6%, and filling both banks another 1.7 us in 82, which together outweighed halving the score stream. Look for the stages where the neighbours are missing (the first and the last sequence), since a round trip that is free in the middle stands bare there. And price each part of a change that "only follows" (the size of a transfer) in every stage where it is on the path, for gain as well as loss.

## What was not expected of the hardware

- Matmuls on different row halves do not keep the program's order: a mask matmul of one half starts at 383.02, ahead of three score matmuls of the other that stand before it in the program and start from 383.08. Four and four issued in turn still start in twos, 14 ns apart.
- 24 transfers of 96 and 32 KB land sooner than 12 of 192 and 64 KB with the same bytes, in packets of 4096 bytes in both: the first half of the first stacks takes 10.3 us instead of 14.5 from its first issue to its last landing.
- Behind one stretch of 2 us in which TensorE was busy 0.47 us, the changed kernel was at the lower level for 13.7 us, though it was busy 8.62 of the 10 us from 656 on; with twelve matmuls without a reader that stay is gone and the last stage is 2.4 us shorter.
